# A fused window-attention, MLP and convolution kernel: the order of the work in a step, and the two layer norms, are moved

## The reference

```python
# block 0: shifted-window attention and an MLP (windows of 7 x 7, shift 3, 3 heads of 32)
xs   = roll(layer_norm(x), (-3, -3))                # first norm
wins = windows(xs)                                  # 49 tokens each
attn = softmax(q @ k.T * scale + rel_bias + mask)
out  = proj(attn @ v), windows undone, rolled back
x    = x + out                                      # x1 in the kernel
y    = fc2(gelu(fc1(layer_norm(x))))                # second norm, hidden width 384
x    = x + y
# block 1: relu, 3x3 depthwise convolution, 1x1 convolution, batch norm
y = pointwise(depthwise(relu(x)) + dw_bias) + pw_bias
y = y * inv + (beta - moving_mean * inv)
```

## Time and profile before

| | us |
|---|---|
| median of 3 runs (6376.44 to 6382.61) | 6379.06 |
| the profiled execution | 6393.57 |
| its span | 6391.8 |
| granted TensorE clock, mean over the span | 0.994 |

### The profile page before, as it was taken

One profiled execution on the slowest core, in us unless ns is written; L12 is line 12 of the kernel. 1 busy time (PEld: TensorE's weight loads), 2 busy tenths in 40 slices (PEclk: granted clock), 3 DMA queues, 4 the chain that ended last, 5 costly groups with the idle time before them and its releaser, 6 DMA issues.

```text
span 6391.8 us, 202888 instructions
## 1 busy us (share of the span) xinstructions
PE 5565.9 (87%) x81186; PEld 3984.3 (62%) x81186; DVE 5516.4 (86%) x13773; ACT 5303.2 (83%) x10784; POOL 3803.8 (60%) x4105
## 2 busy tenths in 40 slices
PE   5888888888888888888888888888888888888887
PEld 3666666666666666666666666666666666666665
DVE  4888888888888888888888888888888888888887
ACT  4888888888888888888888888888888888888886
POOL 2666656666666565655666666566666666566663
PEclk9999999999999999999999999999999999999998
DMA  0111111111111111111111111111111111111110
GB/s 22 27 33 31 31 32 29 33 28 33 28 33 28 33 28 33 29 33 28 33 28 33 28 33 28 33 30 31 32 29 33 28 33 28 33 28 33 30 31 22
DMA packets 275644, 193.69 MB, mean 30 GB/s; under 512 B 229159, under 2 KB 246040, under 8 KB 274712
## 3 DMA queue, kind: packets, MB, share of 16 engines
q1 hardware_dynamic: 274712, 180.70, 10.9%
HBM read 77.81 MB, written 77.07 MB: 24 GB/s over the span
## 4 chain that ended last, share of the span: by engine, by line
POOL 37%; PE 32%; DVE 17%; ACT 9%; issue 3%; SPq 1%; DVEq 0%; DMA 0%; POOLq 0%; ACTq 0%
PE bank L427 15%; POOL xn L944 13%; POOL prob L928 13%; POOL rstd L934 6%; PE bank L511 5%; DVE stats L838 5%; ACT L562 5%; POOL x1n L944 5%; PE bank L408 4%; DVE x L874 4%; PE bank L496 3%; PE bank L523 3%; DVE ssum L798 2%; ACT hT L616 2%; ACT prob L562 2%
## 5 line engine op out<-in xcount | busy, mean ns | idle before, releaser
L822 DVE SCALAR_TENSOR_TENSOR acc<-ymap,taps,acc 96x784 f32<-96x784 f32 (+2 forms) x2176 | 2562.1, 1182 | 45.7
L934 POOL TENSOR_TENSOR rstd<-var_eps,minus_half 112x7 f32<-112x7 f32 x512 | 936.1, 1828 | 2376.7 <-DVE var_eps L853 2376.7
L427 PE MATMUL bank<-x1T,w 96*128 96x448 f32 (+1 forms) x3072 | 1094.3, 506 | 1.9 <-ACT x1T L605 1.9
L446 PE MATMUL bank<-hT,w 128*96 128x448 f32 (+1 forms) x3072 | 1095.8, 492 | 0.0
L616 ACT ACTIVATE hT<-bank,bfc 128x448 f32<-128x448 f32 (+1 forms) x1536 | 883.8, 587 | 175.4 <-PE bank L427 118.3
L944 POOL TENSOR_SCALAR xn<-x_in,minus_mean,rstd 112x96 f32<-112x96 f32 x768 | 853.3, 1121 | 0.0
L928 POOL TENSOR_TENSOR prob<-prob,srec 128x392 f32<-128x392 f32 x768 | 803.3, 1075 | 82.4 <-DVE srec L800 82.4
L919 POOL TENSOR_TENSOR prob<-prob,smax 128x392 f32<-128x392 f32 x768 | 804.3, 1076 | 23.3 <-DVE smax L791 23.3
L427 PEld LDWEIGHTS bank<-x1T,w 96*128 96x128 f32 x3072 | 568.3, 192 | 394.8 <-issue 294.2
L446 PEld LDWEIGHTS bank<-hT,w 128*96 128x96 f32 x3072 | 465.9, 163 | 341.5 <-issue 163.5
L463 PE MATMUL bank<-ident,prob 113*113 113x113 f32 x3072 | 478.1, 278 | 228.0 <-POOL prob L928 220.7
(11 more groups left out here) (99 smaller groups left out, 10777.2 us busy)
## 6 DMA issues: line engine op xcount, KB each, us to landing
out<-o_tile SPq DMA_DIRECT2D x256, 210.0 KB
x_in<-in_x SPq DMA_DIRECT2D x256, 168.0 KB, 3.0
x_in<-in_x SPq DMA_DIRECT2D x256, 126.0 KB, 3.3
k<-qk SPq DMA_DIRECT2D x512, 49.0 KB, 1.9
out<-o_tile SPq DMA_DIRECT2D x256, 84.0 KB
hT<-in_L_conv_rel_bias SPq DMA_DIRECT2D x49, 0.6 KB
x1T<-in_L_conv_fc_w SPq DMA_DIRECT2D x1, 144.0 KB, 2.3
w<-in_L_conv_fc_w SPq DMA_DIRECT2D x1, 144.0 KB, 2.3
```

The source lines that it names most:

```text
L427: pe.matmul(bank[(5, 6, 0)[m]][:, 0:n * PT_], w1[:, m * 128:(m + 1) * 128], x1T[:, first * PT_:(first + n) * PT_], start=True, stop=True). ...
L446: mm = pe.matmul(bank[b][0:C, 0:n * PT_], w2[:, m, :], hT[:, m, first * PT_:(first + n) * PT_], start=False, stop=(m == MC - 1))
L822: last = dve.scalar_tensor_tensor(out=dst, in0=src, scalar=taps[:, i:i + 1], in1=dst, op0=ALU.mult, op1=ALU.add)
L934: pool.tensor_tensor(b["rstd"][:], b["var_eps"][:], minus_half[0:PT_], ALU.pow)\
```

## The change

The order of the steps changes on every engine; nothing is computed otherwise.

- PE: the pointwise convolution (both halves), `turn_x` and `turn_x1` come right after the values, then the softmax transposes and the value weighting of strip t, and the MLP of strip t - 1 last, with `project` between its two `hidden` halves. PSUM banks are dealt out anew; `queries_keys` now waits for `into_map` of the step before, half by half, since it shares banks 3 and 4 with the MLP's result.
- ACT: the exps come right after the keys; then outputs, `x_turned`, `x1_turned`, `probs_turned`, the gelu table, `attention_out`, the gelus, a small exp that loads the exp table, the first norm of strip t + 3, `into_map` first half, the second norm of strip t (no longer t - 1), `into_map` second half.
- DVE: tap 0, both value copies, `add_up` x3, taps 1 to 6, `add_x`, `norm_x` (strip t + 3), taps 7 and 8.
- POOL: `shift` x3, `divide` x3, then root and rest of the second norm of strip t, then root and rest of the first norm of strip t + 3.
- SP: key copies, stores, then the load, of strip t + 4. x1 is held twice, and every engine has one more step at the start.

```diff
-    def steps(eng, step, first=-2):
+    def steps(eng, step, first=-3):
...
-        x1 = sb("x1", PT_, WS, C)
+        x1 = sb("x1", PT_, 2, WS, C)
...
             def load(t, phase):
-                s = t + 3
+                s = t + 4
                 if not has(s):
                     return
-                slot = (phase + 3) % UNROLL
-
-                wait(sp, x1_ready, nth(t - 1, 2, 1))
+                slot = phase
+
+                wait(sp, x1_ready, nth(t, 2, 1))
                 image, k = s // NWIN, s % NWIN
...
             def step(t, phase):
-                load(t, phase)
                 move_keys(t)
                 store(t, phase)
-
+                load(t, phase)
+
+            load(-4, 0)
             load(-3, 1)
             load(-2, 2)
...
                 wait(pe, k_copied, nth(t, 1, 0))
                 wait(pe, k0_moved, 32 * (t + 1))
-                wait(pe, pt_ready, nth(t - 1, 3, 0))
-                wait(pe, ymap_ready, nth(t - 2, 2, 0))
-                wait(pe, out_ready, nth(t - 5, 2, 1))
+                wait(pe, o_ready, nth(t - 1, 1, 0))
+                wait(pe, h_ready, nth(t - 2, 6, 5))
+                if t < 2:
+                    wait(pe, xt_ready, nth(t + 1, 2, 1))
...
                     return
                 wait(pe, xt_ready, nth(t + 1, 2, 1))
                 for u in range(2):
+                    wait(pe, ymap_ready, nth(t - 2, 2, u))
                     pe.matmul(bank[3 + u][:, 0:HALF], wqk[:, u, :], xT[:, u * HALF:(u + 1) * HALF],
...
                     return
-                if i == 0:
-                    wait(pe, ymap_ready, nth(t - 2, 2, 1))
-                else:
-                    wait(pe, q_ready, nth(t + 1, 2, 0))
+                wait(pe, x1_ready, nth(t - 1, 2, i))
+                if t == 0:
...
                 wait(pe, x1n_rest, nth(t - 1, 1, 0))
-                for i, (js, b) in enumerate(((range(4, 7), 0), (range(0, 4), 1))):
-                    if i == 1:
+                for i, (js, b) in enumerate(((range(4, 7), 2), (range(0, 4), 5))):
+                    if i == 0:
+                        wait(pe, s_biased, nth(t, 3, 2))
+                        if not has(t):
+                            wait(pe, h_ready, nth(t - 2, 6, 5))
+                    else:
                         wait(pe, x1n_ready, nth(t - 1, 1, 0))
-                    wait(pe, s_biased, nth(t, 3, i))
-                    if not has(t):
-                        wait(pe, (pt_ready, ymap_ready)[i], (nth(t - 1, 3, 0), nth(t - 2, 2, 0))[i])
+                        wait(pe, k_copied, nth(t + 1, 1, 0))
                     for a, j in enumerate(js):
                         mm = pe.transpose(bank[b][0:C, a * PT_:(a + 1) * PT_], x1n[:, j, :], ident[0:PT_, 0:PT_])
...
+                        wait(pe, xt_ready, nth(t + 2, 2, 1))
                     elif i == 1:
-                        wait(pe, x1_ready, nth(t - 1, 2, 1))
-                    elif i == 2:
                         wait(pe, x1t_ready, nth(t - 1, 2, 0))
-                    else:
+                    elif i > 2:
                         wait(pe, h_ready, nth(t - 1, 6, i - 3))
-                    pe.matmul(bank[(5, 6, 0)[m]][:, 0:n * PT_], w1[:, m * 128:(m + 1) * 128],
+                    pe.matmul(bank[(1, 2, 5)[m]][:, 0:n * PT_], w1[:, m * 128:(m + 1) * 128],
                               x1T[:, first * PT_:(first + n) * PT_], start=True, stop=True).then_inc(h_psum, 1)
             def second_layer(t, half):
                 if not has(t - 1):
                     return
                 first, n = ((0, 4), (4, 3))[half]
...
                 wait(pe, p_ready, nth(t, 3, h))
-                if h == 0:
-                    wait(pe, h_ready, nth(t - 1, 6, 5))
-                elif h == 1:
-                    wait(pe, v_ready, nth(t + 1, 2, 1))
+                if h < 2:
+                    wait(pe, v_ready, nth(t + 1, 2, h))
+                    if not has(t + 1):
+                        wait(pe, x1_ready, nth(t - 1, 2, h))
                 else:
                     wait(pe, out_ready, nth(t - 4, 2, 0))
-                    wait(pe, q_ready, nth(t + 1, 2, 1))
+                    if not has(t - 4):
...
+                    wait(pe, out_ready, nth(t - 4, 2, 1))
+                    if not has(t - 4):
+                        wait(pe, q_ready, nth(t + 1, 2, 1))
                 wait(pe, pt_ready, nth(t, 3, g))
                 for q in range(QUADS):
                     for side in range(2):
...
                 wait(pe, xn_rest, nth(t + 2, 1, 0))
-                for i, (js, perm, b) in enumerate(((range(3, 7), ident[0:PT_, 0:PT_], 3), (range(0, 3), roll[:], 4))):
-                    wait(pe, pt_ready, nth(t, 3, i + 1))
-                    wait(pe, q_ready, nth(t + 1, 2, i))
-                    wait(pe, v_ready, nth(t + 1, 2, 1))
-                    wait(pe, out_ready, nth(t - 4, 2, 0))
+                for i, (js, perm, b) in enumerate(((range(3, 7), ident[0:PT_, 0:PT_], 0), (range(0, 3), roll[:], 1))):
+                    wait(pe, s_biased, nth(t, 3, i))
+                    if t < 0:
+                        wait(pe, xt_ready, nth(t + 1, 2, i))
...
-                if not has(t):
-                    wait(pe, out_ready, nth(t - 5, 2, i))
                 if i == 0:
                     wait(pe, tap_done, nth(t - 4, 9, 8))
-                    wait(pe, q_ready, nth(t + 1, 2, 1))
-                else:
-                    wait(pe, s_biased, nth(t, 3, 2))
+                wait(pe, q_ready, nth(t + 1, 2, i))
+                if not has(t + 1):
+                    wait(pe, ymap_ready, nth(t - 2, 2, i))
+                    wait(pe, out_ready, nth(t - 5, 2, i))
                 for a in range(n):
...
+                pointwise(t, phase, 0)
+                pointwise(t, phase, 1)
+                turn_x(t)
                 turn_x1(t)
-                pointwise(t, phase, 0)
-                hidden(t, 0)
-                hidden(t, 1)
-                second_layer(t, 0)
-                second_layer(t, 1)
                 if has(t):
                     for h in range(HEADS):
                         turn_probs(t, h)
                     for h in range(HEADS):
                         weigh_values(t, phase, h)
-                turn_x(t)
-                pointwise(t, phase, 1)
+                hidden(t, 0)
                 project(t)
+                hidden(t, 1)
+                second_layer(t, 0)
+                second_layer(t, 1)
...
             def step(t, phase):
-                if has(t - 1):
-                    act.activation(table_load[:, 1:2], table_load[:, 0:1], ACT.Gelu_apprx_tanh)
                 queries(t)
                 keys(t)
-                if has(t - 1):
-                    wait(act, x1t_psum, nth(t - 2, 2, 1))
-                    normalise(1, t - 1, x1n, x1, x1n_ready)
-                x1_turned(t)
+                exps(t, 0)
+                exps(t, 1)
                 outputs(t, phase, 0)
-                gelus(t)
-                for g in range(3):
-                    exps(t, g)
-                if has(t + 2):
-                    wait(act, xt_psum, nth(t + 1, 2, 1))
-                    normalise(0, t + 2, xn, x_in[:, (phase + 2) % UNROLL], xn_ready)
-                into_map(t, 0)
-                for h in range(HEADS):
-                    probs_turned(t, h)
-                into_map(t, 1)
-                attention_out(t)
+                exps(t, 2)
                 outputs(t, phase, 1)
                 x_turned(t, 0)
                 x_turned(t, 1)
+                x1_turned(t)
+                for h in range(HEADS):
+                    probs_turned(t, h)
+                if has(t - 1):
+                    act.activation(table_load[:, 1:2], table_load[:, 0:1], ACT.Gelu_apprx_tanh)
+                attention_out(t)
+                gelus(t)
+                if has(t + 1):
+                    act.activation(table_load[:, 1:2], table_load[:, 0:1], ACT.Exp)
+                if has(t + 3):
+                    wait(act, xt_psum, nth(t + 2, 2, 1))
+                    normalise(0, t + 3, xn, x_in[:, (phase + 3) % UNROLL], xn_ready)
+                into_map(t, 0)
+                if has(t):
+                    wait(act, x1t_psum, nth(t - 1, 2, 1))
+                    normalise(1, t, x1n, x1[:, t % 2], x1n_ready)
+                into_map(t, 1)
             steps(act, step)
...
-                if not has(t + 2):
-                    return
-                slot = (phase + 2) % UNROLL
-                wait(dve, xn_ready, nth(t + 1, 1, 0))
-                wait(dve, xn_rest, nth(t + 1, 1, 0))
-                wait(dve, x_loaded[slot], 32 * ((t + 2) // UNROLL + 1))
-                norm_stats(0, t + 2, x_in[:, slot], LN_EPS)
+                s = t + 3
+                if not has(s):
+                    return
+                slot = (phase + 3) % UNROLL
...
             def add_x(t, phase):
                 if not has(t):
                     return
```

(73 more changed lines are left out.)

23 lines of the change are left out of this document (13 added, 10 removed).

## The result

The changed kernel takes 8383.4 us (median of 4, 8373.5 to 8386.2) against 6377.8 before: a ratio of 1.314, 95% interval 1.312 to 1.316. Its span is 8380.0, 1988.2 longer, 7.77 us for each of 256 strips.

The account below looks back on a forecast made before the run. Before, a loop passing from engine to engine bounds the kernel at 24.42 us a step. Alternating steps of 27.8 and 37.2 average 32.5; times 256, plus 140.3 and 1.8, less 14, gives 8450 us, range 7100 to 9400.

Parts of the forecast that it names:

- The loop at full clock: Loop through projection, POOL's roots, ACT's norms and into_map to TensorE's queries: 27.8 us a step against 24.42 before.
- x1 to ACT's norm: From x1 added, through POOL's root, rest and root, to ACT's normalise: 9.4 us, between 8.0 and 10.2.
- rest of x1n: POOL's rest of x1n, ahead of the first norm's root and partly beside taps 7 and 8: 2.6 us.
- ACT's wait: ACT idles some 5 us every step before the first norm, until POOL's offset is ready.
- TensorE's wait: TensorE waits 4.1 us after the scores for ACT's into_map, ahead of the queries.
- TensorE's second wait: TensorE waits again for into_map between the two halves of the queries: 1.75 us.
- Q: Zero point of the step walk: start of the queries' second half on TensorE, reached again 27.8 us later.
- Rival 3: ACT finds the first norm's offset ready if 9.1 us were under 5.3; DVE then sets the pace: 5650 us, chance 0.05.
- The clock: TensorE's clock halves after each long wait, staying low until hidden: 37.2 us steps alternate with 27.8, mean 32.5.
- Rival 1: Clock holds or recovers quickly: 7260 us, chance 0.25; aside, back after the values: 30.7 us a step, 8000 us.
- Rival 2: Slow steps follow each other, the long wait returning in each: 9670 us, or 9180 with four in five slow; chance 0.13.
- What was hidden: SP's key copies, stores and load cost nothing; DVE's later taps have until the next step's pointwise matmuls.

Follow-up runs that it names:

- e1_fill: Changed kernel plus unread matmuls in TensorE's two waits for into_map, five after the scores and two between the query halves: 7263.0 us, 1.139 of the kernel before.
- e6: Changed kernel with DVE's first-norm statistics after tap 1 and POOL's root and rest of the first norm ahead of the second's: 5978.0 us, 0.937 of the kernel before.
- e7: As e6, with ACT also doing both halves of into_map ahead of the second norm: 6018.4 us, 0.942 of the kernel before.
- e5: Changed kernel with both into_map halves ahead of the two norms on ACT and both roots ahead of both rests on POOL: 6030.7 us, 0.945 of before.
- e2_fill_one: Changed kernel plus one unread matmul after the scores and none between the query halves: 8376.5 us, 1.313 of the kernel before.
- e3_map_first: Changed kernel with ACT doing both halves of into_map right after the exp table load, ahead of the two norms: 6907.3 us, 1.085 of the kernel before.
- e8: Changed kernel with POOL's two roots ahead of the two rests and TensorE's two waits filled with unread matmuls: 6864.8 us, 1.075 of the kernel before.

## Why the prediction was right, and where it was not

**Size and sign.** 8450 was forecast for 8383.4, a range of 7100 to 9400, slower at 0.94. The total is closer than its parts deserve, as shown below.

**The loop at full clock: right, and shown.** Forecast 27.8 us a step and 7260 us for the clock held; e1_fill has 27.9 and 7263.0. The terms, in the changed kernel: x1 to ACT's norm 9.45 (forecast 9.4), rest of x1n 2.64 (2.6), ACT's wait 5.2 (5), TensorE's wait 4.29 (4.1). One term is off: TensorE's second wait, between the halves of the queries, was forecast at 1.75 and is 0.50, since the first half takes 1.65 at half clock; Q comes when the map is ready either way. e6 shows the cause, by taking the first norm out from behind x1: the wait and the loss are gone. The chain of waits named in the prediction, POOL's root behind rest behind root, is the one.

**Rival 3 (faster).** The condition it named, an offset ready when ACT comes to it, is what e6 and e7 bring about, and they are faster. With the change as it was made the condition does not hold, as the sum of 9.1 against 5.3 said. The price it named, 5650 us, is not reached: 5978. It took VectorE's 5516.4 us of work as the floor, 21.5 a step. TensorE has more, 5565.9 or 21.7 a step, and with its waits of about 1 us (for the third division 0.89) that makes the 22.6 of e5, e6 and e7.

**The clock: right that it falls at every long wait, wrong on how long it stays down.** The step that failed is "once it has fallen, scores, values and transposes do not soon bring it back", and with it the 37.2 us of a slow step and the alternation of 27.8 and 37.2. In the changed kernel it comes back where turn_x1 ends or where turn_probs ends, 13 to 17 us after it fell and ahead of the hidden layer; the steps show no other kind, 121 of 255 near 31.9 us and 120 near 32.9. So Q to projection is 16.4 or 17.4, not 12.3 or 21; every step is slow by 4.4 us on average, none by 9.4, and none is fast. Since the step has no slow hidden layer, the wait ahead of the queries is there again each time (4.29), and the feedback that was to give every other step its clock back does not occur. Two rivals had a part of this each. Rival 1's aside had the clock back after the values, at 3 us a step and 8000 us in all; it is back a little later, in the transposes, at 4.4. Rival 2 had the long wait return in every step, but at a price of 9.4. The mean of the two wrong lengths, 32.5, falls on the mean of the two right ones, (32.9 + 31.9) / 2 = 32.4: that the total is so near is chance. My evidence was one return of the clock, in hidden, taken for a rule. The kernel before has two more, at its start, and they are in hidden too, so its trace shows no return ahead of hidden:

```profile
135.00:136.00 1.00, 1.00 (x4) 0.79 0.00 0
159.00:160.00 1.00, 1.00 (x5) 0.84 0.00 0
```

From e2_fill_one to e1_fill the lost clock costs (8376.5 - 7263.0) / 7263.0 = 15%: it is paid once a step, 256 times. The Trainium skill ("TensorE: Matmul & The Clock Gate", section "What's actually happening") has the ramp penalty under 1% of a typical kernel span. The measurement decides.

**What was hidden stayed hidden.** SP's queue, the divisions and taps 1 to 6 set nothing at full clock: in e1_fill TensorE's wait for the third division is 0.89, as before the change, DVE stands 0.63 before x1, so the taps are done by then, and the projection is 12.3 after Q where 12.2 was forecast.

## What to carry to other kernels

When a stage is moved forward in every engine's queue, look at what now stands behind it in the last engine of the loop: here two engines' queues (POOL: root, rest, root; ACT: norm, map) put a result that was long ready, the map, behind one that could not be ready, at 3.4 us a step. Work that depends on nothing late (a norm of a strip three ahead) belongs in front of work that depends on this step, on each engine that serves it. And a wait of a few us on TensorE can cost twice, once itself and once in the clock of what follows (here 4.4 us a step); filling it with matmuls that nobody reads tells the two apart in one run.

## What the runs showed of the hardware that I had not expected

- Matmuls that do nothing made a kernel 13% faster (e2_fill_one 8376.5, e1_fill 7263.0), by the granted clock alone (0.766 to 0.993).
- The clock also falls without a long wait: in e3_map_first after waits of 1.37, 0.16 and 0.89 us within 6 us, in most steps, and costs 3.2 us there (27.3 against 24.1). In the kernel before, steps with waits of 0.9 to 1.1 nearly all kept it; it fell at 3009 to 3010 (granted 0.72) behind a wait of 1.54. In e7, steps with waits of 0.16 and 0.89 keep it as a rule.
- GpSimd's power of 112 x 7 takes 1.48 us, and 2.2 beside a tap on VectorE (e8, e6); in e1_fill, beside statistics or the bias additions, 1.48. The kernel before has both: 1.48, and 2.20 for the first norm's root at 3055.92, beside tap 3. The Trainium skill ("GPSIMD Engine Reference", section "8. Key points") says that GpSimd shares its SBUF interfaces with VectorE and that they contend when VectorE's instruction has two inputs in SBUF, which a tap has; the rows agree.
